# Graph network in two layers on one core: fewer semaphore increments from TensorE, and messages ahead of ranks in the edge loop

## The reference

```python
# layer L0: d = edge_weight, row = src, col = dst
env = 0.5 * (cos(d * pi / 10) + 1) * (d < 10)
r = exp(-0.5 * ((d[:, None] - centers) / (abs(widths) + 1e-5)) ** 2) * env[:, None]
r = silu(r @ rbf_w1 + rbf_b1) @ rbf_w2 + rbf_b2
W = silu(r @ filt_w1 + filt_b1)
W = silu(W @ filt_w2 + filt_b2) @ filt_w3 + filt_b3
msg = (x[col] @ node_w + node_b) * W
h = x + segment_sum(msg, row)
out = layernorm(h) * ln_g + ln_b
x = layernorm(x + out * sigmoid(out @ gate_w + gate_b))
# layer L1, two halves of 128 features
x_fwd = segment_sum(w * x[col, :128], row) / clip(deg_row, 1)
x_bwd = segment_sum(w * x[row, 128:], col) / clip(deg_col, 1)
x = layernorm(x + concatenate([x_fwd, x_bwd]))
```

## Time and profile before

| | us |
|---|---|
| median of three runs | 6022.33 (6012.38 to 6031.83) |
| the profiled execution | 6008.27 |
| its span | 6006.5 |
| PE, PEld busy in the span | 3694.8, 2677.7 |
| DVE, ACT, POOL busy | 2377.6, 1607.1, 3415.2 |

### The profile page before, as it was taken

How to read it: one execution, slowest core, us unless ns; L and a number is a source line. 1 busy time by engine, 2 the same in 40 slices (tenths; PEclk the granted TensorE clock), 3 DMA queues, 4 the chain that set the end, 5 groups by cost and what they waited for, 6 DMA issues and landing times. The chain is left out here.

```text
span 6006.5 us, 76202 instructions
## 1 busy us (share of the span) xinstructions
PE 3694.8 (62%) x16356; PEld 2677.7 (45%) x16357; DVE 2377.6 (40%) x7105; ACT 1607.1 (27%) x4212; POOL 3415.2 (57%) x3664
## 2 busy tenths in 40 slices
PE   7777777777777777777799833333332444455444
PEld 5444444444444444444588632222222444444443
DVE  5434434344344443334233622221222445555457
ACT  4333333333333333333366611111111000000000
POOL 2455555554555555555576566666666666566665
PEclk9888888888888888888899966656665667777776
DMA  7333333332333333332499311111111333333334
GB/s 217 94 97 98 95 97 101 95 101 90 94 97 95 95 97 100 98 99 91 131 296 295 120 48 43 44 44 45 44 44 44 99 84 85 84 85 84 84 85 90
DMA packets 460154, 590.18 MB, mean 98 GB/s; under 512 B 65457, under 2 KB 380849, under 8 KB 460081
## 3 DMA queue, kind: packets, MB, share of 16 engines
q0 software_dynamic: 128512, 318.04, 17.5%
q1 hardware_dynamic: 331584, 271.50, 15.6%
HBM read 392.61 MB, written 197.07 MB: 98 GB/s over the span
## 5 line engine op out<-in xcount | busy, mean ns | idle before, releaser
L533 POOL DMA_INDIRECT s_rows<-arena,adr x784 | 770.6, 983 | 1118.4 <-issue 1095.7
L978 PE MATMUL ps<-arena,f2s 128*128 128x512 f32 x1568 | 864.3, 702 | 427.5 <-ACT arena L642 335.3
L573 POOL DMA_INDIRECT d_rows<-arena,adr x832 | 809.5, 973 | 501.1 <-issue 243.6
L586 POOL DMA_INDIRECT arena<-x_half,idx x832 | 800.9, 963 | 507.1 <-issue 230.9
L525 POOL DMA_INDIRECT arena<-y_rows,idx x784 | 758.0, 967 | 305.3 <-issue 227.0
L989 PE MATMUL ps<-f3s,arena 128*128 128x256 f32 x3136 | 800.2, 406 | 171.0 <-issue 112.8
L1166 PE MATMUL ps<-arena 128*128 128x128 f32 x1664 | 376.9, 397 | 649.7 <-DVE arena L1559 566.8
L989 PEld LDWEIGHTS ps<-f3s,arena 128*128 128x128 f32 x3136 | 632.5, 204 | 306.7 <-issue 130.0
L978 PEld LDWEIGHTS ps<-arena,f2s 128*128 128x128 f32 x1568 | 349.8, 229 | 854.1 <-issue 472.1
L1328 DVE TENSOR_TENSOR arena<-arena,ps 128x392 f32<-128x392 bf16 x196 | 109.6, 559 | 1448.1 <-remote 1338.1
L1166 PEld LDWEIGHTS ps<-arena 128*128 128x128 f32 x1664 | 325.6, 292 | 692.7 <-issue 691.5
(11 more groups left out here) (217 smaller groups left out, 5073.0 us busy)
## 6 DMA issues: line engine op xcount, KB each, us to landing
arena<-s_rows SPq DMA_DIRECT2D x104, 1048.0 KB, 5.7
arena<-d_rows SPq DMA_DIRECT2D x52, 1040.0 KB
arena<-de_rows SPq DMA_DIRECT2D x392, 128.0 KB
d_rows<-arena,adr POOLq DMA_INDIRECT x832
arena<-x_half,idx POOLq DMA_INDIRECT x832
s_rows<-tpl_s SPq DMA_DIRECT2D x98, 131.0 KB
arena<-y_rows,idx POOLq DMA_INDIRECT x784
s_rows<-arena,adr POOLq DMA_INDIRECT x784
```

Of the source, the lines that this page charges most:

```text
L533: pool.indirect_dma_start(s_rows, bass.IndirectOffsetOnAxis(ap=adr[b][:, t:t + 1], axis=0), msg[b][:, t, :], None).then_inc(scattered[b], 16)
L573: pool.indirect_dma_start(d_rows, bass.IndirectOffsetOnAxis(ap=adr2[b][:, t:t + 1], axis=0), drow[b][:, t, :], None).then_inc(scattered_d[ ...
L586: pool.indirect_dma_start(gath2[b][:, t, :], None, x1_half, bass.IndirectOffsetOnAxis(ap=idx2[b][:, t:t + 1], axis=0)).then_inc(gathered2[ ...
L978: last = mm(ps[:, 3 + m, :], f2s[:, k, m * P:(m + 1) * P], s2[:, k, :], start=(k == 0), stop=(k == 1))
```

## The change

In the edge loop TensorE increments `ahead_mm` once for layer23, ranks and layer1 together, `l4_mm` once, and `l5_mm` twice as before. DVE's order becomes radial_basis(g+2), messages(g-1), product and ranked(g+2), one_hot_rank(g+3). ACT does silu1(g+2) ahead of radial(g+3), whose wait for `rbf_done` goes. In L1's back half `back_mm` is incremented once, after spread and the turn three groups on; in the forth half `turns_mm` once, after both sums. Waits name group counts in place of tile counts. `ends4` holds a block's end in groups. Names of the counts are worked out by small functions.

```diff
+        def layer1_of(g):
+            return g + 1
+        def ranks_of(g):
+            return g + 1
+        def layer23_of(g):
+            return g + 2
+        def turned_of(g):
+            return g + 1
+        def spread_of(g):
+            return g + 3 if fixed(g) and g < EARLY else g + 4
+        def returned_of(d):
+            return 1 + (d // 2 + 1 if fixed(d) and d < 2 * LEAD else d - LEAD + 1)
...
             def radial(g, q, b):
                 act.wait_ge(de_in[b], 32 * q + 32)
                 if not (fixed(g) and g == 0):
                     act.wait_ge(tanh_done, g)
-                if not (fixed(g) and g < 2):
-                    act.wait_ge(rbf_done, g - 1)
...
-                act.wait_ge(l4_mm, 2 * g + m + 1)
+                if m == 0:
+                    act.wait_ge(l4_mm, g + 1)
...
                 if ahead(g, 1):
                     silu2(g + 1)
+                if ahead(g, 2):
+                    silu1(g + 2, b)
                 if ahead(g, 3):
                     radial(g + 3, q + (b + 3) // 4, (b + 3) % 4)
-                if ahead(g, 2):
-                    silu1(g + 2, b)
...
             def pe_group(g, q, b):
                 layer4(g)
                 if ahead(g, 1):
-                    layer23(g + 1, b + 1)
+                    last = layer23(g + 1, b + 1)
                 if ahead(g, 2):
                     rank_step(g + 2, b)
-                    layer1(g + 2, b)
+                    last = layer1(g + 2, b)
+                if ahead(g, 1):
+                    last.then_inc(ahead_mm, 1)
...
             def pe_back(g, q, b):
-                spread_rows(g, b)
+                last = spread_rows(g, b)
                 if not fixed(g) or g + 3 < G1:
-                    turn(g + 3, b + 3)
+                    last = turn(g + 3, b + 3)
+                last.then_inc(back_mm, 1)
...
             def sum_rows(g, q, b):
-                sum_forth(g, q, b)
+                last = sum_forth(g, q, b)
                 if fixed(g) and g < LEAD:
                     for d in (2 * g, 2 * g + 1):
-                        sum_back(d, d // 8, d % 8)
+                        last = sum_back(d, d // 8, d % 8)
                 elif not fixed(g) or g + LEAD < G1:
-                    sum_back(g + LEAD, q + (b + LEAD) // 8, (b + LEAD) % 8)
+                    last = sum_back(g + LEAD, q + (b + LEAD) // 8, (b + LEAD) % 8)
+                last.then_inc(turns_mm, 1)
...
             def dve_group(g, q, b):
                 if ahead(g, 2):
+                    radial_basis(g + 2, b + 2)
+                if not (fixed(g) and g == 0):
+                    for h in range(2):
+                        messages(g - 1, q + (b + 3) // 4 - 1, (b + 3) % 4, h)
+                if ahead(g, 2):
                     product(g + 2, b)
                     ranked(g + 2, b)
                 if ahead(g, 3):
                     one_hot_rank(g + 3, b + 1)
-                    radial_basis(g + 3, b + 3)
-                if not (fixed(g) and g == 0):
-                    for h in range(2):
-                        messages(g - 1, q + (b + 3) // 4 - 1, (b + 3) % 4, h)
...
             def sums_back(g, b):
                 places = places_of(mybir.EngineType.DVE, 1, g, ACW)
+                dve.wait_ge(turns_mm, returned_of(g))
                 for t in range(GT):
                     if not (fixed(g) and g == 0 and t == 0):
                         dve.wait_ge(addedd, GT * g + t)
-                    dve.wait_ge(aggd_mm, 2 * g + t // 2 + 1)
```

More of the change, by code:

```diff
@@ L107, in build @@
         ends = sb("ends", [P, NB], i32)
+        ends4 = sb("ends4", [P, NB], i32)
         ntc = sb("ntc", [NB, 2])
@@ L474, in load_back @@
                 if not (fixed(c) and c < 2):
-                    sp.wait_ge(aggd_mm, 8 * c - 8)
+                    sp.wait_ge(turns_mm, returned_of((CT // GT) * (c - 1) - 1))
                 sp.dma_start(d_buf[b], d_v[:, bass.ds(c * CT, CT), :]).then_inc(d_in[b], 16)
-            loop(sp, load_back, SC, 2, 2, 0)
+            loop(sp, load_back, SC, 2, 8, 0)
             for c in range(CHUNKS):
@@ L778, in turned_out @@
             def turned_out(g, b):
-                act.wait_ge(turned_mm, g + 1)
-                if not (fixed(g) and g < 4):
-                    act.wait_ge(spread_mm, g - 3)
+                act.wait_ge(back_mm, turned_of(g))
                 A(hot_t[b % 4], ps[:, turn_bank(g, b), 0:GT * P // 2].bitcast(bf16), ACT.Copy).then_inc(hott_done, 1)
@@ L830, in forth_out @@
             def forth_out(n):
-                last_tile = act.value_load(ends[0:1, n:n + 1], min_val=1, max_val=ST + 1)
-                act.wait_ge(aggf_mm, last_tile)
+                last_turn = act.value_load(ends4[0:1, n:n + 1], min_val=1, max_val=G1 + 1)
+                act.wait_ge(turns_mm, last_turn)
                 A(agg[:, n * H:n * H + HALF], ps[:, n % SLOTS, 0:HALF], ACT.Copy,
@@ L950, in rank_step @@
                        skip_group_check=True)
-                mm(ps[:, 7, 0:GT * NB2], before_b[:, :], cur, start=False, stop=False,
-                   skip_group_check=True).then_inc(rank_mm, 1)
+                return mm(ps[:, 7, 0:GT * NB2], before_b[:, :], cur, start=False, stop=False, skip_group_check=True)
             pe.wait_ge(bases_set, 1)
@@ L960, in layer1 @@
                 pe.wait_ge(rbf_done, g + 1)
-                mm(ps[:, 0, 0:GW], w1d[:, :], rbf[b % 2], start=True, stop=True).then_inc(l1_mm, 1)
+                return mm(ps[:, 0, 0:GW], w1d[:, :], rbf[b % 2], start=True, stop=True)
             def layer23(g, b):
@@ L969, in layer23 @@
                                   s1[b % 2][h * R:(h + 1) * R, :], start=True, stop=True)
-                last.then_inc(l23_mm, 1)
+                return last
             def layer4(g):
@@ L979, in layer4 @@
                                   start=(k == 0), stop=(k == 1))
-                    last.then_inc(l4_mm, 1)
+                last.then_inc(l4_mm, 1)
             def layer5(g, b):
@@ L1010, in _ @@
             rank_step(0, 0)
-            layer1(0, 0)
+            layer1(0, 0).then_inc(ahead_mm, 1)
             pe.wait_ge(s1_done, 1)
@@ L1105, in turn @@
                         ident_b[:, :])
-                last.then_inc(turned_mm, 1)
+                return last
             def spread_rows(g, b):
@@ L1130, in _ @@
                     pe.wait_ge(slot_free, SLOTS + NB)
-                    turn(0, 0)
-                    turn(1, 1)
+                    turn(0, 0).then_inc(back_mm, 1)
+                    turn(1, 1).then_inc(back_mm, 1)
                 pe.wait_ge(x1_set, c - 1)
@@ L1135, in _ @@
                     spread_rows(g, g)
-                    turn(g + 2, g + 2)
+                    turn(g + 2, g + 2).then_inc(back_mm, 1)
             pe.wait_ge(x1_set, CHUNKS)
-            turn(EARLY + 2, EARLY + 2)
+            turn(EARLY + 2, EARLY + 2).then_inc(back_mm, 1)
             loop(pe, pe_back, G1, RING, 2 * RING, RING, EARLY)
@@ L1156, in sum_back @@
                               d_buf[b // 4][:, (b % 4) * GT + t, 0:ACW], start=True, stop=True)
-                    if t % 2:
-                        last.then_inc(aggd_mm, 1)
+                return last
             def sum_forth(g, q, b):
@@ L1165, in sum_forth @@
                 for t in range(GT):
-                    mm(forth[:, bass.ds(at[t], HALF)], hot_f[b][:, t, :], gath2[b][:, t, :],
-                       start=False, stop=False, skip_group_check=True).then_inc(aggf_mm, 1)
+                    last = mm(forth[:, bass.ds(at[t], HALF)], hot_f[b][:, t, :], gath2[b][:, t, :],
+                              start=False, stop=False, skip_group_check=True)
+                return last
             def sum_rows(g, q, b):
-                sum_forth(g, q, b)
+                last = sum_forth(g, q, b)
                 if fixed(g) and g < LEAD:
                     for d in (2 * g, 2 * g + 1):
-                        sum_back(d, d // 8, d % 8)
+                        last = sum_back(d, d // 8, d % 8)
                 elif not fixed(g) or g + LEAD < G1:
-                    sum_back(g + LEAD, q + (b + LEAD) // 8, (b + LEAD) % 8)
+                    last = sum_back(g + LEAD, q + (b + LEAD) // 8, (b + LEAD) % 8)
+                last.then_inc(turns_mm, 1)
             loop(pe, sum_rows, G1, 8, 16, 16)
@@ L1281, in starts @@
                     step(V.memset(ends[:, NB - 1:NB], ST + 1))
+                    step(V.tensor_scalar(ends4[:, :], start[:, :], float(2 * GT - 1), None, ALU.add))
+                    step(V.tensor_scalar(ends4[:, :], ends4[:, :], GT.bit_length() - 1, None, ALU.logical_shift_right))
+                    step(V.memset(ends4[:, NB - 1:NB], G1 + 1))
                 step(V.tensor_tensor(start[:, :], start[:, :], tot[:, :], ALU.subtract))
```

34 lines of the change are left out of this document (16 added, 18 removed).

## The result

The changed kernel takes 5777.8 us (median of 4 runs, 5759.1 to 5803.5); the kernel before, run beside it on the same chip, 6017.4 (4 runs, 6007.9 to 6031.8). The ratio is 0.961, interval 0.958 to 0.963: 240 us faster. That is 124 us above the forecast of 5654, inside the range, and 7 us from the rival "only the order counts" (5785).

What follows compares the result with a forecast made beforehand. POOL's indirect transfers come in bursts, and what ends its pauses, TensorE increments seen late, sets the time. Terms of -237, -45 and -86 sum to -368 from 6008.27: 5640, plus 14 gives 5654 us; range 5290 to 6080.

Steps and rivals of the forecast that it cites:

- only the order counts: Rival: the number of increments gives nothing, only the edge loop's new order does; 5785 us, chance 0.21.
- Messages first, -237 us: Edge loop: DVE's messages start at the release, ahead of the product; 14.71 to 13.5 us a group over 196 groups.
- The number of increments in the edge loop, nothing: Edge loop: four TensorE increments for seven, priced at nothing beyond the 13.5 us; at most 4.5 us a group.
- The rule that I quoted: Trainium skill: eight copies take equally long with a semaphore after each or one after the last; applied to TensorE, 5785.
- silu2 behind ranks and layer1, nothing: Edge loop, ACT: silu2 also waits for ranks and layer1, 1.4 us more, covered by layer5's 3.5 us of TensorE.
- Slower, TensorE idle once a group: Rival, edge loop: TensorE idles once a group, returns at low clock, 16.3 us a group; whole 6203 us, chance 0.14.
- L1's back half, -45 us: One increment for turn and spread; a quarter of POOL's 194 us wait for staged addresses goes, bounds 0 and -194.
- forth half, -86 us: L1: one increment for six; a third of POOL's 257 us excess idle time goes, bounds +125 and -257.
- Messages at the release ahead of the product: Sign for the forecast, edge loop timeline: DVE's messages start at the release before the product, POOL follows 2.3 us later.
- The scatters' idle time down by about 200: Sign for the forecast, edge loop: POOL's idle time ahead of the message scatters falls by about 200 us.
- Long bursts followed by short ones: Sign for the forecast, edge loop: POOL's long cycle, 25.5 us for two groups, followed by a short one of 14.2.
- DVE's wait moved to the messages with the same 1200 us: Sign against the forecast, edge loop: DVE's remote wait moves from the product to the messages, the same 1200 us.

Runs made afterwards that it cites:

- e1: The changed kernel with VectorE's edge-loop order of the kernel before (messages last), four increments a group kept: ratio 0.987 to the kernel before.
- e2: The changed kernel with the edge loop's seven increments and ACT's order of the kernel before, messages still ahead: ratio 0.946 to the kernel before, 5611.6 us.
- g2: The changed kernel with DVE's messages moved behind product, ranked and one-hots, radial basis still first: ratio 0.974 to the kernel before.
- e3: The changed kernel with nine more TensorE increments a group that nobody waits for, thirteen instead of four: ratio 0.961 to the kernel before, 5707 us.
- f1: The changed kernel run again, unaltered, on a chip that holds increments back: ratio 0.962 to the kernel before, 5784.5 us.
- f2: The changed kernel with layer23 given its own increment, so silu2 doesn't wait for ranks and layer1: ratio 0.957 to the kernel before, 5751.3 us.
- r_after: The changed kernel run again, unaltered, on a chip that holds nothing back: ratio 1.0019 to the kernel before, which takes 4682.4 us there.
- g1: The changed kernel with one of four gathers a group from the fifth group on, work left out: ratio 0.846 to the kernel before, 5029.4 us.

## Why the prediction was right, and where not

**Messages first, -237 us.** The edge loop measured -243, but that is the whole change there and not DVE's order by itself. That the order is the main cause is shown: without it the change brings 1.3% (e1), with it 3.9%, with the order and nothing merged in the edge loop 5.4% (e2), and moving the product back in front of the messages loses 1.4 points (g2). So the order is worth 2.6 points on top of the rest of the change, and with that rest undone 5.4 but for the little of L1, some 320 us of 6017. The rest of the change gains 1.3 points with the old order (e1) and costs 1.5 with the new (e2 against e3); why it turns was not tested. That these parts add up to the -237 forecast for one of them is luck. The form was wrong too. I built 13.5 us from a long cycle of 25.5 alternating with a short one of 14.2; what came is a row of short ones of 13.3 us. I had named that case ("short ones alone 13.6 to 14.2") and put the number between, so the number was not worked out from what came. What I missed is that DVE's stop at the product is what makes a long cycle: DVE is held there while the messages of a finished layer5 stand behind, and POOL gets two groups' work only when all has drained. With the messages first, POOL's next group needs layer5's increments alone. That last sentence is read from the cycles of after and g2, and was not tested by itself. The stretch that I gave for the forecast alone, 5540 to 5760, doesn't follow from its own bounds: 13.2 us with 200 of L1 give 5526, 14.0 with 60 give 5823, and 5778 lies inside.

**The number of increments in the edge loop, nothing.** Right, and shown for the new order of DVE: 13 a group run as 4 do (e3). The rule that I quoted from the Trainium skill, VectorE: DVE Perf Modes, The DRAIN you can't avoid, holds in its outcome for TensorE here.

**silu2 behind ranks and layer1, nothing.** This step failed in part. The prediction said that 1.4 us more would lie in layer5's 3.5. In the cycle above silu2 starts at 1516.09 behind layer1; in e2 it starts before layer1 and 3.3 us earlier than the matmul that the change would have it wait for:

```profile
1310.94 1.26 ACT L665 ACTIVATE arena<-ps,b 128x512 f32<-128x512 f32 x2
...
1314.26 1.22 PE L983 MATMUL ps<-arena,w1d 128*128 128x256 f32 x2 [1.43 <-DVE arena L1397]
...
1315.52 0.47 ACT L660 ACTIVATE arena<-ps,col 128x256 f32<-128x256 f32 x1 [3.31 <-issue]
```

The extra wait is not 1.4 us of ranks and layer1. Among these TensorE waits for the one-hots (L966) and for the radial basis (L982), which I had costed apart; in the change, one cycle further on:

```profile
1524.87 1.32 DVE L1349 TENSOR_SCALAR arena<-lane,arena 128x49 bf16<-128x49 f32 x8
...
1526.24 0.34 PE L966 MATMUL ps<-arena,after_b 128*128 128x392 bf16 x1 [2.25 <-DVE arena L1349]
...
1528.69 1.22 PE L982 MATMUL ps<-arena,w1d 128*128 128x256 f32 x2 [1.27 <-DVE arena L1398]
```

silu2 inherits both. The prediction had the one-hots done 3.7 us after layer5; here they end at 1526.19, 6.7 after it, because the second half of the messages ahead of them is itself held. silu2's share is 33 us (f1 against f2), where e2 and e3 lie 96 apart. In these single cycles layer4 follows layer5 at once with either; in which cycles the time is lost I have not found.

**Slower, TensorE idle once a group.** Its time did not come, though TensorE does stand idle at the ranks in 101 of some 178 groups, 1.8 us each. The clock of the edge loop rose from 0.86 to 0.88, and layer4 takes 3.60 us in the cycle of after, not the 6.53 of the earlier trace rows.

**L1's back half, -45 us; forth half, -86 us.** Both mis-sized: -7 and -1. These two terms are 123 us too large, against a miss of 124. POOL's wait for staged addresses went from 194.1 to 176.9 where I had taken 45 off, and `gather2`'s "remote" rose from 163.2 to 182.4 where I had said below 100. Both terms were fractions, a quarter and a third, of a pause that I ascribed to the number of increments. e3 showed in the edge loop that the number buys nothing; for L1 there is only before against after, since every other kernel on a chip that holds increments back has L1's part of the change in it. The same two halves in r_after show what the pause goes with: where nothing is held back, `gather2`'s idle time is 262.2 us, nearly all its own 0.30 a transfer. I take it for the holding back itself, which the change does not touch. I should have applied to L1 the value that I took for the edge loop, nothing; then the sum is 5785.

**What was to be seen.** Messages at the release ahead of the product: yes, and POOL follows 1.7 us after the held half. The scatters' idle time down by about 200: 258. Long bursts followed by short ones: no. Of the signs against me, TensorE at layer1 (L982) waits 68.5 us in 56 stops for the radial basis and 102.1 in 95 for "issue", 1.1 us a stop in most groups; that sign came, and the kernel is faster all the same. DVE's wait moved to the messages with the same 1200 us, which I had named as a sign against me: it did move, with 1287 us, and the kernel is still faster. It was a poor sign, since DVE waits there for layer5 also where nothing is held: r_after has, from 300 to 2000,

```profile
DVE arena L1406 <- PE ps L1010: 652.5, 332, 3.5
```

2.0 us a stop, against 3.8 after. Two such stops a group make 3.6 us more, about what a group is longer there (13.45 us against 10.2), so the stop says that the loop is slower and not what makes it so.

## What to carry to other kernels

Where an increment can be seen late, ask of every waiting instruction not how long it waits but what stands behind it on its engine: put first the one whose result the bottleneck (here POOL) wants, and what only feeds later groups behind it. Don't merge increments to save their number: with the new order it saved nothing here, and merging makes the early consumer wait for the last producer and all that this one waits for. Giving silu2 its own increment back gained some 33 us, and the kernel with nothing merged in the edge loop, and ACT's old order, was the best. A pause whose cause a change does not touch is to be priced at nothing, and not at a fraction of itself.

## What the runs showed of the hardware

While POOL's indirect transfers run, some of TensorE's increments are seen late, the ranks' 15 us in the earlier trace rows, and mostly come through soon after the last transfer. Of DVE's "remote" stops in the edge loop, 67 of 76 at the product before ended 2.1 to 3.2 us after it, and 101 of 116 at the messages after 0.8 to 2.5. The others ended within a burst, and some increments are seen at once there (silu2 at 1516.09), so "held until all has drained" is not the whole rule; which increment is held is open. With five transfers a group instead of eight no wait in the edge loop was "remote", while L1 went on as before (g1).

This does not occur on each chip. The kernel before took 6017, 5934, 6016 and 5941 us on four chips or visits, and 4682 on another, where the change's run showed POOL with little idle time but its own 0.30 us a transfer; the change is worth 3.9% where it was timed on the former and costs 0.2% on the latter. What makes a chip hold increments back is open, and no run here was made to find it.
